# Delta-rule attention on one Trainium2 core: decayed K transposed through DRAM and VectorE instead of TensorE, a new order of steps, and the last FFN group spread over the first projections

## What is computed

```python
xn = layernorm(x) * ln_w + ln_b
q, k, v = xn @ Wq.T, xn @ Wk.T, xn @ Wv.T           # 16 heads of 64
alpha, aR = sigmoid(xn @ Wa.T + ba), sigmoid(xn @ WaR.T + baR)
beta, gamma = sigmoid(xn @ Wb.T + bb), sigmoid(xn @ Wg.T + bg)
def step(S, R):                                      # 256 tokens, one after the other
    kn = k_t / norm(k_t)
    r = clip(v_t - S.T @ kn, -1, 1)
    S = alpha_t * S;  S = S + beta_t * outer(kn, v_t - kn @ S)
    R = aR_t * R;     R = R + gamma_t * outer(kn, r - kn @ R)
    o_t = S.T @ q_t + R.T @ q_t
attn = o @ Wo.T
h = silu(x @ w1 * s1) * (x @ w2 * s2)                # FFN, 512 hidden units
h = gelu(h @ h1 * sh1); h = gelu(h @ h2 * sh2); ffn = h @ w3 * s3
```

## Time and profile before

| | before |
|---|---|
| median of 3 runs | 2342.6 us (2341.97 to 2350.55) |
| the profiled execution: its time | 2340.6 us |
| the profiled execution: span from first to last instruction | 2338.5 us |
| busy: PE, weight loads, DVE, ACT, POOL | 97%, 82%, 72%, 53%, 51% |
| granted TensorE clock, mean over the span | 0.987 |
| attention, from the first projection to the end | 341.4 to 2338.5 us |

### The profile page before, as it was taken

The page is one execution under the profiler, slowest core; times in us unless marked ns, Lnnn a source line. Parts: engine busy times, 40 slices in busy tenths (PEclk is TensorE's granted clock), DMA queues, the critical chain, the costliest instruction groups (busy, mean ns, idle before and its releaser), DMA issues.

```text
span 2338.5 us, 120262 instructions
## 1 busy us (share of the span) xinstructions
PE 2266.3 (97%) x52544; PEld 1909.1 (82%) x52544; DVE 1692.4 (72%) x3727; ACT 1240.2 (53%) x2391; POOL 1189.3 (51%) x2384
## 2 busy tenths in 40 slices
PE   8999996999999999999999999999999999999997
PEld 3454544898888888988888898898898998888887
DVE  5411017888888788888888888888887888888874
ACT  3333236555555555555555655555565555555540
POOL 0010006666656655666666566666665666666641
PEclk9999997999999999999999999999999999999999
DMA  3000001221112222222112121111212222222221
GB/s 92 0 1 0 21 1 20 42 39 39 37 36 39 46 39 42 39 40 39 38 37 49 38 42 39 37 35 38 39 36 50 39 42 43 44 41 41 42 46 25
DMA packets 306501, 84.92 MB, mean 36 GB/s; under 512 B 280384, under 2 KB 303040, under 8 KB 305984
## 3 DMA queue, kind: packets, MB, share of 16 engines
q1 hardware_dynamic: 304784, 74.89, 16.3%
q10 hardware_dynamic: 1200, 2.36, 0.3%
HBM read 41.53 MB, written 35.65 MB: 33 GB/s over the span
## 4 chain that ended last, share of the span: by engine, by line
PE 91%; DMA 3%; POOL 2%; issue 1%; DVE 1%; SPq 1%; ACT 1%; POOLq 0%; ACTq 0%; DVEq 0%
PE bank L516 12%; PE bank L392 5%; PE bank L539 5%; PE bank L530 5%; PE bank L405 5%; PE bank L496 4%; PE bank L560 3%; PE bank L551 3%; PE bank L478 3%; PE bank L675 3%; PE bank L467 3%; PE bank L616 3%; PE bank L473 3%; PE bank L485 3%; PE bank L458 3%; PE bank L593 3%
## 5 line engine op out<-in xcount | busy, mean ns | idle before, releaser
L1144 POOL TENSOR_TENSOR lane_t<-lane_n,lane_x 128x15 f32<-128x15 f32 (+7 forms) x960 | 318.8, 332 | 371.7 <-DMA lane_n<-n_dram 301.5
L1147 POOL TENSOR_TENSOR lane_x<-lane_x,lane_t 128x15 f32<-128x15 f32 (+7 forms) x960 | 335.6, 350 | 75.2
L516 PE MATMUL bank<-kq,Kt 64*64 64x96 f32 x8192 | 361.5, 232 | 0.6
L516 PEld LDWEIGHTS bank<-kq,Kt 64*64 64x64 f32 x8192 | 315.2, 135 | 3.4 <-issue 3.3
L1343 ACT ACTIVATE oS<-bank 128x512 f32<-128x512 f32 x64 | 38.2, 597 | 351.9 <-PE bank L664 351.9
L1118 POOL TENSOR_TENSOR KQF<-efull,kn 128x768 f32<-128x768 f32 x64 | 124.3, 1942 | 186.4 <-ACT efull L1298 186.4
L1267 ACT ACTIVATE ea<-bank,nba 128x256 f32<-128x256 f32 x256 | 107.5, 471 | 193.1 <-PE bank L478 136.9
L1320 ACT ACTIVATE kend<-Kt,ek 128x64 f32<-128x64 f32 x768 | 189.8, 341 | 0.0
L924 DVE COPY_PREDICATED AS<-cst,bank 128x384 f32<-128x384 int32 x256 | 142.6, 582 | 31.1 <-PE bank L516 28.3
L873 DVE TENSOR_TENSOR_SCAN cum<-rst,dk 128x512 f32<-128x512 f32 x128 | 153.5, 1241 | 0.2
L1129 POOL TENSOR_TENSOR Kt<-ek,kn 128x512 f32<-128x512 f32 x64 | 115.5, 1805 | 71.1 <-ACT ek L1311 71.1
(11 more groups left out here) (158 smaller groups left out, 6338.4 us busy)
## 6 DMA issues: line engine op xcount, KB each, us to landing
XF<-x_dram SPq DMA_DIRECT2D x256, 64.0 KB, 2.3
lane_n<-n_dram SPq DMA_DIRECT2D x128, 124.0 KB, 2.8
x_dram<-lane_x SPq DMA_DIRECT2D x128, 124.0 KB, 2.4
n_dram<-AS SPq DMA_DIRECT2D x256, 32.0 KB, 2.0
n_dram<-AR SPq DMA_DIRECT2D x256, 32.0 KB, 1.7
wt<-in_win SPq DMA_DIRECT2D x4, 640.0 KB, 4.9
out_y<-acc SPq DMA_DIRECT2D x16, 128.0 KB, 2.0
hw<-in_h1T SPq DMA_DIRECT2D x1, 1024.0 KB, 11.7
```

Source lines behind the costliest of these rows:

```text
L516: ins = pe.matmul(v3(dst[hd[h], o:o + kinds * C], kinds)[:, :, i * SUB:(i + 1) * SUB], Kt[hd[h], m * 96 + i * SUB:m * 96 + i * SUB + C], r ...
L1144: pool.tensor_tensor(tv, lane_n[:, m * SUB + m + 1:m * SUB + BASE].unsqueeze(2).to_broadcast([L, rows, m + 1]), xv[:, m, 0:m + 1].unsqueez ...
L1147: pool.tensor_tensor(xv[:, m + 1:, 0:m + 1], xv[:, m + 1:, 0:m + 1], tv, ALU.subtract).then_inc(s["lane_step"], 1)
```

## The change

- `turn_kend` and `copy_kend` are gone. `to_end` writes `kend` in another arrangement of its columns (two halves of 32 apart); SP writes it to DRAM (`keys_out`, one DMA), reads it back with the blocks on other partitions (`keys_in`, four DMAs), and DVE transposes 32x32 blocks (`turn_keys`). `kendT` has two buffers instead of three.
- The order of the steps is new on all engines. The loop of POOL and of SP starts elsewhere (`small_inverses(k+2)` at the end of POOL's turn; on SP `lanes_out(k+1)` first, then the weights, `wo`, `store`, `blocks_out(k+2)`, `keys_out`, `lanes_in`, `keys_in(k+1)`). On ACT `log_decay` is now next to each `gate`.
- Attention starts when the first layer of the last FFN group is done. Its second layer is placed behind the projections of quad 0, its third behind those of quad 1, its last behind `project_v(1)`, in the banks 4 to 6.
- Buffers are laid out anew so that those of attention that are written early don't lie over FFN's; a few steps wait for `ffn_added` instead.

```diff
+            def keys_out(n):
+                need(sp, "kend", n + 1)
+                need(sp, "k_in", (n - 1) * 4 * 16)
+                sp.dma_start(k_dram[n % 2].rearrange("e d t -> (e d) t"), kend[:, :]).then_inc(s["k_out"], 16)
+            def keys_in(n):
+                need(sp, "k_out", (n + 1) * 16)
+                need(sp, "kT", n)
+                for h in range(2):
+                    for j in range(2):
+                        e = 2 * h + j
+                        sp.dma_start(v3(kend_in[e * SUB:(e + 1) * SUB, :], 2),
+                                     k_dram[n % 2, 2 * h:2 * h + 2, :, j * 2 * (T - C):(j + 1) * 2 * (T - C)].rearrange("i d t -> d i t")).then_inc(s["k_in"], 16)
...
 -                    blocks_out(k + 2, 0)
-                    blocks_out(k + 2, 1)
-                    lanes_in(k + 2)
-                    lanes_out(k + 2)
-                if on(k + 5) and (k + 5) % B == 0:
-                    load_weights(k + 5)
+                if l:
+                    lanes_out(k + 1)
+                if on(k + 4) and (k + 4) % B == 0:
+                    load_weights(k + 4)
...
+                    blocks_out(k + 2, 0)
+                    blocks_out(k + 2, 1)
+                    keys_out(k + 2)
+                    lanes_in(k + 2)
+                if l:
+                    keys_in(k + 1)
...
-            pe.wait_ge(s["ffn_added"], GROUPS)
+            pe.wait_ge(s["h1_sb"], 4 * GROUPS)
+            pe.wait_ge(s["down_used"], GROUPS - 1)
+            def late_second(o):
+                for k in range(4):
+                    ins = pe.matmul(bank[4 + o][:, :], hw1[:, k * HID + o * P:k * HID + (o + 1) * P], hA[:, k * FFN_TOK:(k + 1) * FFN_TOK], start=(k == 0), stop=(k == 3))
+                ins.then_inc(s["g1_ps"], 1)
...
             def project_kq(n):
                 need(pe, "w_loaded", (n // B + 1) * 16)
-                need(pe, "kT_sb", 2 * (n - 1))
                 need(pe, "kn", n)
                 need(pe, "vt_sb", n)
...
+                if n == 0:
+                    late_second(0)
+                elif n == 1:
+                    late_third(0)
...
+            def turn_keys(n):                 # dve
+                need(dve, "k_in", (n + 1) * 4 * 16)
+                need(dve, "rs_ps", 3 * (n - 1))
+                dve.transpose(v4(kendT[n % 2][:, :], 12, 2).rearrange("p m i d -> p i m d"), v4(kend_in[:, :], 2, 12)).then_inc(s["kT"], 1)
```

More of the change, by code:

```diff
@@ L73 @@
     "kk": "k's operands", "kp": "k's operands of the predictions", "qq": "q's operands", "kf": "k against the state", "ea1": "one over S's gate", "kfull": "operands against the state",
-    "kend": "k decayed to the chunk's end", "kT_ps": "turned in PSUM (2)", "kT_sb": "turned in SBUF (2)",
+    "kend": "k decayed to the chunk's end", "k_out": "it is in DRAM", "k_in": "back with its halves of tokens on partitions (4 DMAs)", "kT": "turned",
     "pr_ps": "products in PSUM (6 a quad)", "pr_sb": "masked in SBUF (6 a quad)", "n_sb": "N times beta or gamma (2 a quad)",
@@ L695, in body @@
                 if e:
-                    s_s(k - 1, 2)
+                    r_s(k - 1, 1)
+                    s_p(k - 1, 2)
                 if d:
@@ L1061, in body @@
                 if e:
-                    s_state(k - 1, 2)
+                    r_state(k - 1, 1)
+                    s_clip(k - 1, 2)
                 if b:
@@ L1089, in body @@
                     running_sums(k + 3, 0)
-                    running_sums(k + 3, 1)
+                if d:
+                    turn_keys(k)
                 if e:
                     r_state(k - 1, 2)
+                    s_clip(k - 1, 3)
+                if d:
+                    level1(k)
+                if a:
+                    clamp_r(k + 3)
+                if d:
+                    s_solved(k, 0)
+                if b:
+                    mask_products(k + 2, 0)
+                if e:
+                    r_right(k - 1, 3)
+                if a:
+                    clamp_norms(k + 3)
+                if d:
+                    s_state(k, 0)
+                if e:
+                    r_solved(k - 1, 3)
+                if d:
+                    s_clip(k, 0)
+                if b:
+                    mask_products(k + 2, 1)
+                    mask_products(k + 2, 2)
+                if d:
+                    r_solved(k, 0)
+                    s_right(k, 1)
+                if a:
+                    norm_k(k + 3)
+                    running_sums(k + 3, 1)
+                if d:
+                    s_solved(k, 1)
+                if b:
+                    mask_products(k + 2, 3)
+                if d:
+                    s_state(k, 1)
+                    r_state(k, 0)
+                if b:
+                    scale_blocks(k + 2, 0)
+                if a:
+                    from_anchors(k + 3)
+                if d:
+                    s_clip(k, 1)
+                if e:
+                    add_out(k - 1)
+                if b:
+                    mask_products(k + 2, 4)
+                if d:
+                    r_right(k, 1)
+                    s_right(k, 2)
+                if b:
+                    mask_products(k + 2, 5)
+                if d:
+                    s_solved(k, 2)
+                if b:
+                    scale_blocks(k + 2, 1)
+                if a:
+                    operands_q(k + 3)
+                if d:
+                    r_solved(k, 1)
+                    s_state(k, 2)
             for k in range(-3, LAST + 3):
```

373 lines of the change are left out of this document (174 added, 199 removed).

## The result

The changed kernel takes 2270.7 us in the median of five executions (2259.9 to 2275.5), the kernel before, run beside it, 2342.0 us (2336.8 to 2350.6). The ratio is 0.969, with a 95% interval of 0.966 to 0.972: 3.1% faster. The forecast of 2282 us lies 0.5% above the median.

The account below looks back on a forecast made before the run. TensorE's matmul issue bounds attention. Start 405.5, sixty turns of 28.6 (1716), gaps 18, reloads 18.6, stalls 7, rest 115: span 2280, time 2282 us (2262 to 2302; 8 in 10: 2247 to 2326).

Parts of the forecast that it names:

- The floor and the turn: TensorE's pieces summed to a floor of 28.2 us a turn without waits; with waits 28.6, against 29.74 before.
- What leaves TensorE is gained, as long as no other engine is late: Attention is bound by matmul issue on TensorE, so removing turn_kend's 1.53 us a turn is gained.
- seven trips against six: Returns from full-array matmuls to smaller ones on TensorE, 0.15 us each: seven a turn in the new order, six before.
- The wait at `s_s(k,1)`: Walking one turn, the chain from norms takes 5.9 us, TensorE has 5.6 us to issue: it waits 0.3 us.
- VectorE's slack: With turn_keys VectorE keeps 3 us of 5, nearly all early in its turn, none between s_clip(k,0) and s_solved(k,2).
- The table loads: On ScalarE, logarithms and exponentials alternate four times a turn instead of twice: two more loads of 1283 ns, no drain.
- The way through DRAM: Loop of SP, DRAM and POOL needs 26.5 to 28.5 us; keys land 1.5 to 2 us early; priced at nothing.
- The reload: At three weight reloads project_kq stalls some 4.5 us, with half clock 6.2 us each: 18.6 us instead of 5.2.
- The gaps and stalls: Short unexplained TensorE gaps of 0.3 us a turn, 18 us in sixty, plus two other stalls of 7 us together.
- The start: Attention starts during FFN's last group; level0_nx(0) comes at 405.5 instead of 409.07 us, full-length turns from there.
- VectorE becomes the bound: Rival, chance 0.20: VectorE at 90% load and blocked by POOL makes the turn 29.3 us, time 2324 us.
- The way through DRAM sets the turn: Rival, chance 0.07: each microsecond the keys land beyond their margin costs 60 us; 3 us beyond gives 2462 us.

Follow-up runs that it names:

- the run with the copies: The changed kernel with eight more 96 KB DRAM-to-DRAM copies a turn in SyncE's queue ahead of the four DMAs of keys_in: 2570.1 us, ratio 1.100.
- the three kernels in which it did: Kernel before with K^T through DRAM, key DMAs ahead of blocks_out (2591.7 us) or placed as in the change (3040.8); changed kernel with eight 96 KB copies more (2570.1).

## Why the prediction was right, and where it was not

The time: 2282 us forecast, 2270.7 in the median and 2259.9 in the profiled execution, whose clock (0.987) was the highest of the five (the others 0.979 to 0.983). Against the profiled span I was 22 us too high: 2.3 too low at the start, 21.3 too high in the turns and 3.1 in the tail.

- **The floor and the turn.** 28.6 forecast; 28.72 and 28.57 read at one place, but 28.40 as the shortest turn, which is the like of the 29.74 that I started from. So the undisturbed turn is 0.2 us shorter than forecast, 12 us in sixty. The pieces of the floor add up to 28.1 and 29.5 us, not 28.2 and 29.6, which moves nothing that follows. That TensorE's issue bounds the new order was right: 24 products that take 1.40 us lengthen the shortest turn by 1.40 us, the whole replacement of `turn_kend` costs 0.1 us.
- **What leaves TensorE is gained, as long as no other engine is late.** This is the step that did not hold where it seemed safest, in the kernel before: there the same removal costs 0.27 us a turn instead of giving 1.53: it uncovers a wait of 0.77 us for `s_clip`, and brings GpSimd and VectorE together for 1.02 us. I charged the order of steps seven trips against six, 0.15 us, and took the condition as given. Of the 1.33 us a turn between the two kernels, the old order without `turn_kend` gives -0.27, and the new order without the way through DRAM lies 1.70 below that, and the way takes 0.10 back. The new order does not pay alone: with as many products more as `turn_kend` has, its turn is 30.81 us, above the 30.23 of before. The removal pays in full only with it. That the new order had a product group in `turn_kend`'s place was no argument of mine; the forecast came out since I walked the turn of the new order itself and did not take 1.53 off the old one.
- **The wait at `s_s(k,1)`.** 0.3 forecast, 0.06 read: the walk was 0.24 us too long there, and the stretch has no slack, so a longer `norm_k` goes through to the turn, 0.72 of 0.75 us.
- **VectorE's slack.** It exists where I said, but swallows only 0.6 of 1.0 us, not nearly all.
- **The table loads.** Four a turn, 1283 ns, the next instruction 0.02 us behind, as in the earlier trace rows. The Trainium skill (ScalarE: Activation LUTs, What ACT_TABLE_LOAD costs) adds a drain; no load here shows one, and the 30.6 us a turn that it gave did not come.
- **The way through DRAM.** Priced at nothing, costs 0.1 us a turn. The margin, 1.5 to 2 us by the walk, is 2.0 us in the turn that I read and 2.2 in the median of 57; the run with the copies shows some 3.5 us covered in all, VectorE's slack included.
- **The reload.** 18.6 us forecast. The three waits are 2.5, 2.5 and 1.7 us, 6.7 in all, and only one has a half clock behind it: some 8.4 us. The mis-sized term is the single wait, 4.5 us. `wt` landed 4.2 us after its issue at 781.14 us, and TensorE had 1.8 us to do meanwhile; I had charged nearly the whole landing and the clock each time.
- **The gaps and stalls.** I carried 0.3 us a turn and two stalls over from before, 25 us. In place of the two stalls (7 us) the first full turn is 5.2 us too long, for another reason. The gaps are still there: without the three turns at the reloads the mean is 28.76 us, 0.36 over the shortest, and before it was 30.08 without the two long turns, 0.34 over 29.74. Their cause is as unknown as it was. The turns came out 21 us below the forecast by the shorter undisturbed turn (12 us) and the reloads (10 us).
- **The start.** `level0_nx(0)` forecast at 405.5, read at 407.8; `project_kq(1)` at 340.4 (341 forecast) and `scale_blocks(0,1)` at 379.2 (379). The walk of the start was right, but I ended it at `level0_nx(0)`, as if turns had their full speed from there. The first one is 5.2 us longer, with the clock at 0.60. I counted 3.6 us for the spread of FFN's last group; the whole times show no gain (0.969 with it, 0.970 without).
- **The rivals.** *VectorE becomes the bound* is refuted by the run without `turn_keys` (0.1, not 0.95 us a turn), though the meeting it rests on took place (`scale_blocks(·,1)` 1197 ns). *The way through DRAM sets the turn* did not happen, but the three kernels in which it did took 4 to 11 us a turn more, a part of it by the lower clock.

## What to carry to other kernels

An operation taken out of the bounding engine gives its time only if the next input is there by then, and if what stood beside it keeps its place. Here half of `turn_kend` covered a wait for VectorE, and `copy_kend` on ScalarE kept GpSimd away from a long VectorE instruction; taking both out cost more than it gave. So walk the turn of the new order with all queues, and look in it for two long elementwise instructions of VectorE and GpSimd that may meet. The price of more work on an engine that isn't the bound is read from the place where it stands, not from the engine's share. A start that is pulled forward is only won if the whole time shows it. And compare the shortest and the mean turn, with the granted clock beside them, before a longer turn is laid to one wait.

## What the runs showed of the hardware

- VectorE and GpSimd hold each other up when both run elementwise operations with two inputs: `operands_q` took 2.32 instead of 1.21 us while `far_half` ran on GpSimd, and one wait that kept them apart made the kernel 2.8% faster (2367.2 to 2301.4 us). I knew the effect from the earlier trace rows, but not that it decides over the sign of a change. The Trainium skill (SBUF — State Buffer, SBUF: two separate sides) says that the two share a pair of ports by an exclusive lock, so that the later one stands still until the other is done. These rows agree: `far_half` ended at 1513.54 us and `operands_q` 1.08 us later, near its own 1.21 us.
- The issue of a DMA on SyncE is not a fixed price: in the changed kernel 0.39 us in the mean for `keys_out`, 0.46 for the blocks of AR, 0.60 for `keys_in`; 0.79 us each in the row of eight copies of 96 KB from DRAM to DRAM shown above, 5.0 to 7.3 us for the eight in 49 turns.
- After much the same idle times, the seven kernels with the changed start had a granted clock of 0.50 to 0.90 over the 20 us from 410 us on, and a first full turn of 29.7 to 38.3 us. One trace does not tell what a change at such a place is worth.
- Where TensorE waited 2 to 3 us in each turn for a late input, its granted clock fell too: in the run with the copies 0.84 to 0.95 in most turns, which were 2 to 3 us longer than those at full clock.
